# Values made token by token, and loaded through ScalarE's queue after the last weighted sums

## The reference, cut to what matters

```python
q = (xn @ wq + bq).reshape(b, n, H, HD).transpose(0, 2, 1, 3)    # H = HD = 16, k and v alike
fq, fk = jax.nn.elu(q) + 1.0, jax.nn.elu(k) + 1.0
kv = jnp.einsum('bhnd,bhne->bnde', fk, v)                         # per token n: 16 x 16
qkv = jnp.einsum('bhnd,bnde->bhne', fq, kv)
attn = qkv / (jnp.einsum('bhnd,bnd->bhn', fq, fk.sum(axis=1))[..., None] + 1e-06)
x = q_x + attn.reshape(b, n, c) @ wo + bo
return x + gelu(_ln(x) @ fc_w + fc_b) @ proj_w + proj_b
```

## Time and profile before

| | us |
|---|---|
| timed runs, median of 3 | 1108.08 |
| the profiled execution, its own time | 1103.53 |
| its span | 1101.4 |
| PE matmuls busy | 959.7 (87%) |
| DVE busy | 648.7 (59%) |
| ACT busy | 491.6 (45%) |
| GpSimd busy | 184.4 (17%) |
| DMA, mean over the 16 engines, queue of SP | 44.3% of the span, 353552 packets |
| DMA, queue of ACT | 2.9% of the span, 6656 packets |

### The profile page before, as it was taken

The page is one execution under the profiler, slowest core; times in us unless marked ns, Lnnn a source line. Parts: engine busy times, 40 slices in busy tenths (PEclk is TensorE's granted clock), DMA queues, the critical chain, the costliest instruction groups (busy, mean ns, idle before and its releaser), DMA issues.

```text
span 1101.4 us, 29193 instructions
## 1 busy us (share of the span) xinstructions
PE 959.7 (87%) x12208; PEld 716.9 (65%) x12208; DVE 648.7 (59%) x1557; ACT 491.6 (45%) x770; POOL 184.4 (17%) x113
## 2 busy tenths in 40 slices
PE   3755797989798989999999899999999899897966
PEld 1433685858595857777676758686776768685733
DVE  2433446565565666566667666766656765657433
ACT  1233354545354543646455444646464454342422
POOL 2020121121213121212121211211121210203000
PEclk9958699989898989999999999999999899898989
DMA  4556254545545453645555545637464535331023
GB/s 173 109 106 141 48 107 102 114 109 107 115 93 130 93 130 91 148 108 137 118 119 127 117 100 119 142 96 160 96 150 104 130 71 129 93 88 45 33 77 115
DMA packets 360343, 120.88 MB, mean 110 GB/s; under 512 B 325520, under 2 KB 342160, under 8 KB 359952
## 3 DMA queue, kind: packets, MB, share of 16 engines
q1 hardware_dynamic: 353552, 108.47, 44.3%
q10 hardware_dynamic: 6656, 10.50, 2.9%
HBM read 60.20 MB, written 58.72 MB: 108 GB/s over the span
## 4 chain that ended last, share of the span: by engine, by line
PE 64%; issue 10%; SPq 9%; DVE 8%; DMA 5%; ACT 2%; POOL 2%; ACTq 0%; DVEq 0%; POOLq 0%
PE pw L922 15%; PE pj L906 12%; PE ps L859 8%; PE ps L878 6%; SPq L338 6%; PE pw L832 5%; PE pj L832 4%; PE ps L891 4%; PE ps L970 3%; PE pw L859 3%; SPq L350 2%; PE pj L1014 2%; DMA scratch_nd<-ot 2%; DVE nd L679 1%; DVE am L650 1%
## 5 line engine op out<-in xcount | busy, mean ns | idle before, releaser
L922 PE MATMUL pw<-hT,w_fc 128*128 128x512 f32 x768 | 213.6, 419 | 11.1 <-DVE hT L670 11.1
L906 PE MATMUL pj<-w_pj,hidden 128*128 128x256 f32 x1536 | 208.4, 285 | 3.9 <-DVE hidden L663 3.9
L906 PEld LDWEIGHTS pj<-w_pj,hidden 128*128 128x128 f32 x1536 | 197.1, 189 | 15.3 <-DVE hidden L663 5.1
L505 ACT ACTIVATE xhT<-pw,col 128x512 f32<-128x512 f32 x128 | 88.0, 687 | 229.3 <-PE pw L922 227.9
L663 DVE TENSOR_TENSOR hidden<-xhT,hidden 128x512 fp32r<-128x512 f32 x128 | 88.5, 692 | 168.8 <-ACT hidden L506 168.8
L922 PEld LDWEIGHTS pw<-hT,w_fc 128*128 128x128 f32 x768 | 144.8, 200 | 44.0 <-DVE hT L670 12.8
L859 PE MATMUL ps<-xhT,w_qkv 128*128 128x512 f32 x256 | 126.1, 639 | 3.4 <-ACT xhT L459 3.2
L650 DVE TENSOR_TENSOR am<-ps,mask 128x512 f32<-128x512 f32 x128 | 79.4, 682 | 66.0 <-PE ps L878 66.0
L878 PE MATMUL ps<-kq 16*64 16x64 f32 x4096 | 89.2, 314 | 28.3 <-issue 15.2
L878 PEld LDWEIGHTS ps<-kq 16*64 16x64 f32 x4096 | 77.9, 209 | 50.9 <-issue 48.6
L859 PEld LDWEIGHTS ps<-xhT,w_qkv 128*128 128x128 f32 x256 | 51.4, 208 | 62.1 <-issue 60.4
(11 more groups left out here) (105 smaller groups left out, 1170.4 us busy)
## 6 DMA issues: line engine op xcount, KB each, us to landing
scratch_nd<-ot SPq DMA_DIRECT2D x32, 512.0 KB, 4.3
nd<-scratch_nd SPq DMA_DIRECT2D x96, 128.0 KB, 2.8
x_sb<-in_x SPq DMA_DIRECT2D x16, 512.0 KB, 5.8
scratch_v<-feat_v ACTq DMA_DIRECT2D x16, 512.0 KB, 3.8
scratch_q<-fqk SPq DMA_DIRECT2D x32, 256.0 KB, 3.6
scratch_k<-fqk SPq DMA_DIRECT2D x32, 256.0 KB, 4.7
kq<-scratch_q SPq DMA_DIRECT2D x128, 64.0 KB, 2.8
kq<-scratch_k SPq DMA_DIRECT2D x128, 64.0 KB, 2.8
```

The source lines that it names most:

```text
L505: nc.scalar.activation(gelub[:, u], pw[u], ACT.Gelu, bias=b_fc[:, m:m + 1])
L906: last = nc.tensor.matmul(pj[u][:, D * s:D * (s + 1)], hidden[:, m % SLOTS, a, lo:lo + P], w_pj[:, b, m], start=(m == 0 and n == 0 and s = ...
L922: last = nc.tensor.matmul(pw[bank], w_fc[:, b, c, P * m:P * (m + 1)], hT[:, a, c], start=(n == 0), stop=(n == len(order) - 1))
```

## The change

DV now puts 128 tokens on the partitions and 256 channels in the columns: 8 products of 256 columns in place of 4 of 512. DVE adds the bias as a row `bv`, made once by the new stage WV at the start, and ACT issues two stores. The row of a token in DRAM is chosen so that 8 DMAs of 1024 pieces of 64 bytes, issued by ACT, bring the values straight into `vb`. VL moves from SP's queue behind NS0 to ACT, between M3 (and NS1) and M4. VT, `vd` and their copies are gone. The DRAM buffer is doubled (`VRING`), and the weighted sums of round 1 wait for `v_in` on PE. In iteration 1, VL still stands ahead of DV; in iteration 2 it stands behind B3 and NS1.

```diff
-MERGED = ["L", "XS", "M1", "J2", "Y", "NS0", "VL", "M2", "NL0", "K0", "DS", "Z", "M3", "NS1", "D1", "M4", "NL1", "N0", "K1"]
+MERGED = ["L", "XS", "M1", "J2", "Y", "NS0", "M2", "NL0", "K0", "DS", "Z", "M3", "NS1", "VL", "D1", "M4", "NL1", "N0", "K1"]
-    yield 0, ["DS:0", "L:1", "D1", "X", "DV", ...
-    yield 1, ["X", "K0", "WS", "VL", "DV", "DQ", "DS:2", "DK", "D1:2", "B0", "B8", "VT", "K1"]
+    yield 0, ["WV", "DS:0", "L:1", "D1", "X", "DV", ...
+    yield 1, ["X", "K0", "WS", "VL", "DV", "DQ", "DS:2", "DK", "D1:2", "B0", "B8", "K1"]
...
 # SP
-                if p.stage == "VL":
-                    ...
-                    for j in range(NQ):
-                        for b in range(2):
-                            for v in range(2):
-                                sp.dma_start(vd[2 * j + b::2 * NQ]..., src[j, b, v]).then_inc(S["v_in"], 16)
 # ACT, stage DV
-                    for m in range(NC):
-                        wait(f"sa_full{m}", at(f"sa_full{m}", 1))
-                        nc.scalar.activation(feat_v[:, m], sa[m], ACT.Identity, bias=...).then_inc(S[f"sa_free{m}"], 1)
-                    act.dma_start(v_dram.rearrange("(c p) t -> p c t", p=P), feat_v[:, :, :]).then_inc(S["v_out"], 16)
+                    wait("v_in", at("v_in", -INC["v_in"]["VL"]))
+                    for u in range(2):
+                        wait(f"sa_free{u}", at(f"sa_free{u}", 1))
+                    dst = v_dram[p.t % VRING].rearrange("(g n b k) d -> b n g (k d)", g=2 * TA, n=2 * NQ, k=SUB)
+                    for b in range(2):
+                        act.dma_start(dst[b], feat_v[b::2].rearrange("p s d -> p (s d)")).then_inc(S["v_out"], 16)
+                if p.stage == "VL":
+                    wait("v_out", at("v_out"))
+                    for v in range(2):
+                        wait(f"sa_full{v}", at(f"sa_full{v}"))
+                    src = v_dram[p.t % VRING].rearrange("(g n) (h d) -> g h n d", g=2 * TA, d=HD)
+                    for v in range(2):
+                        for a in range(TA):
+                            act.dma_start(vb[BLOCK * v + a:BLOCK * (v + 1):TA, :, 0:HD], src[TA * v + a]).then_inc(S["v_in"], 16)
-                if p.stage == "VT":
-                    ...
 # DVE
+                if p.stage == "WV":
+                    dve.wait_ge(w_in[1], 16)
+                    for c in range(NC):
+                        last = nc.vector.tensor_copy(pb128[:, c], b_qkv[:, 2 * NC + c:2 * NC + c + 1].broadcast_to([P, P]))
+                    ...
+                    nc.vector.tensor_copy(bv[:, :], pw[0][:, 0:D]).then_inc(S["pw_free0"], 1)
+                if p.stage == "DV":
+                    ...
+                    for u in range(2):
+                        wait(f"sa_full{u}", at(f"sa_full{u}", 1))
+                        nc.vector.tensor_tensor(feat_v[:, 2 * u:2 * u + 2], sa[u].rearrange("p (s d) -> p s d", d=D),
+                                                bv[:, :].unsqueeze(1).broadcast_to([P, 2, D]),
+                                                ALU.add).then_inc(S[f"sa_free{u}"], 1)
 # PE
+                if p.stage == "DV":
+                    for u in range(2):
+                        wait(f"sa_free{u}", at(f"sa_free{u}"))
+                        for s in range(2):
+                            for c in range(NC):
+                                last = nc.tensor.matmul(sa[u][:, D * s:D * (s + 1)], xhT[:, c, 2 * u + s::SUB], w_qkv[:, 2, c],
+                                                        start=(c == 0), stop=(c == NC - 1))
+                        last.then_inc(S[f"sa_full{u}"], 1)
-                if p.stage == "VT":
-                    ...
-                            last = nc.tensor.transpose(pw[u][:, P * g:P * (g + 1)], vd[:, KG // 2 * u + g::KG], ident[:, :])
 # PE, round M1
-                        empty("pw")
+                        wait("v_in", at("v_in"))
                         weighted(0)
```

More of the change, by code:

```diff
@@ L22 @@
 X2RING = 1
+VRING = 2
 SLOTS = 4
@@ L58, in iterations @@
 def iterations():
[L60 to L62 removed]
+    yield 0, ["WV", "DS:0", "L:1", "D1", "X", "DV", "DS:1", "DQ", "L:2", "D1:1", "DK"]
+    yield 1, ["X", "K0", "WS", "VL", "DV", "DQ", "DS:2", "DK", "D1:2", "B0", "B8", "K1"]
+    yield 2, ["K0", "Y", "B1", "NS0", "X", "DV", "B2", "NL0", "DQ", "B3", "NS1", "VL", "NL1", "N0", "K1",
               "DK", "YB", "N", "A2", "R", "SA", "B0", "B8", "H"]
@@ L69, in iterations @@
         yield i, MERGED + (HEAD_TAIL if i % PER_BATCH == PER_BATCH - 1 else FULL_TAIL)
-    yield 16, ["XS", "M1", "J2", "Y", "NS0", "VL", "M2", "NL0", "K0", "Z", "M3", "NS1", "M4", "NL1", "N0", "K1", "XL",
-               "J7", "JA", "YB", "E", "VT", "N", "F1", "F3", "F4", "A2", "R", "SA", "B0", "B8", "H", "FX", "F2"]
+    yield 16, ["XS", "M1", "J2", "Y", "NS0", "M2", "NL0", "K0", "Z", "M3", "NS1", "VL", "M4", "NL1", "N0", "K1", "XL",
+               "J7", "JA", "YB", "E", "N", "F1", "F3", "F4", "A2", "R", "SA", "B0", "B8", "H", "FX", "F2"]
     yield 17, ["XS", "M1", "J2", "Y", "NS0", "M2", "NL0", "Z", "M3", "NS1", "M4", "NL1", "N0", "XL",
@@ L327, in run @@
                                          ).then_inc(S[f"{c}_out"], 16)
-                if p.stage == "VL":
[L329 to L334, removed]
-                    for j in range(NQ):
-                        for b in range(2):
-                            for v in range(2):
-                                sp.dma_start(vd[2 * j + b::2 * NQ].rearrange("p (v h t) -> p v h t", v=2, h=H)[:, v],
-                                             src[j, b, v]).then_inc(S["v_in"], 16)
                 if p.stage in ("K0", "K1"):
@@ L484, in run @@
                                              bias=b_qkv[:, j:j + 1]).then_inc(S[full.replace("full", "free")], 1)
-                if p.stage == "VT":
-                    for u in range(2):
-                        wait(f"pw_full{u}", at(f"pw_full{u}", 1))
-                        src = pw[u][:, :].rearrange("p (g d j) -> p j g d", d=HD, j=2 * NQ)
-                        dst = vb[:, :, :].rearrange("p (j g) e -> p j g e", j=2 * NQ)[:, :, KG // 2 * u:KG // 2 * (u + 1), 0:HD]
-                        nc.scalar.activation(dst, src, ACT.Identity).then_inc(S[f"pw_free{u}"], 1)
                 if p.stage == "H":
@@ L844, in run @@
                     last.then_inc(S["pw_full0"], 1)
+                if p.stage == "WV":
+                    wait("bv_ready", at("bv_ready", 1))
+                    for c in range(NC):
+                        last = nc.tensor.matmul(pw[0][:, P * c:P * (c + 1)], pb128[:, c], ident[:, :], start=True, stop=True)
+                    last.then_inc(S["pw_full0"], 1)
                 if p.stage == "X":
@@ L861, in run @@
                         last.then_inc(S[full], 1)
-                if p.stage == "VT":
-                    wait("v_in", at("v_in"))
-                    for u in range(2):
-                        wait(f"pw_free{u}", at(f"pw_free{u}"))
-                        for g in range(KG // 2):
-                            last = nc.tensor.transpose(pw[u][:, P * g:P * (g + 1)], vd[:, KG // 2 * u + g::KG], ident[:, :])
-                        last.then_inc(S[f"pw_full{u}"], 1)
                 def scores(b, part):
```

65 lines of the change are left out of this document (34 added, 31 removed).

## The result

The changed kernel takes 1187.14 us (median of 4 runs, 1181.42 to 1189.14) where the kernel before took 1108.16 beside it. The ratio is 1.0702, with a 95% interval from 1.0663 to 1.074. The forecast was 1117.5 with a range up to 1140, so the direction was right and the size far off. The span of the profiled execution grew from 1101.4 to 1184.3 us.

What follows compares the result with a forecast made beforehand. PE was taken to bound full iterations, with SP's value-load issues in the chain early on. The terms 28.0 - 7.9 - 2.0 - 5.0 - 3.7 gave +9.4 us, so 1117.5 us, range 1092 to 1140.

Steps and rivals of the forecast that it cites:

- V: Time of VL's 8 issues on ACT behind M3, taken as 5.4 us, with an upper end of about 7.3.
- s = V - 3.4: PE's stall in M4 from VL's issue time on ACT: 2.0 us in each of 14 rounds, +28.0 us.
- The rival of cheap issues: VL's 8 issues on ACT take 3.8 us, PE stalls 0.4 a round: -13 us, 1095; chance 0.33.
- The DMA-bound rival: DMA engines bound VL's issues: 7.3 us, PE stalls 3.9 a round, +36 us, 1144; chance 0.18.
- a few falls, 2 us each: Granted clock may fall after a short PE stall; a few falls, 2 us each, counted only in the DMA-bound rival.
- N takes 4.55 us as today: On DVE, N starts when JA ends, takes 4.55 us; first add ends 0.3 us ahead of DK's need; cost 0.
- The rival of a late division: VL's packets delay N's load, N starts 2 us late, DK waits for DVE's add: +4 us, 1112; chance 0.09.
- VT: Transposes taken off PE: 0.88 us in each of nine full iterations, -7.9 us.
- DV's weight loads: Twice as many on PE, each under a matmul of 256 columns: 0, at most +0.2 us a tile.
- Iterations 0 to 2: Mainly ACT's shorter wait before iteration 1's exponentials, 6.2 us: together -5 us, between -7 and -2.
- Iterations 3 to 6: DVE's 3.4 us wait for N's load goes, adds and stores take nearly all back: -0.5 each, -2 us.
- Iteration 16: N's wait of 3.98 us for its load goes, as the load comes earlier: -3.7 us.

Runs made afterwards that it cites:

- e2: Changed kernel with VL, still issued by ACT, moved from behind M3 to behind stage X; 1112.27 us, ratio 1.0112 to the kernel before.
- e3: Changed kernel with VL's 8 DMAs carrying 256 pieces each in place of 1024, three quarters of the values not loaded; 1144.75 us, ratio 1.0374.
- e10: Kernel before, plus 8 DMAs of 256 pieces of 64 bytes issued by ACT behind M3 into an unread tile; 1118.42 us, ratio 1.0136.
- e11: e2 with GpSimd's two additions of YB waiting until N is done; 1093.66 us, ratio 0.9925 to the kernel before.
- e9: e7 with DV's stationary operand read as 128 neighbouring tokens, not every fourth (result not computed correctly); 1085.62 us, ratio 0.9864.
- e7: Changed kernel with VL issued by ACT behind X and DV ahead of N on DVE; 1088.98 us, ratio 0.9873 to the kernel before.
- e12: e7 with VL in 2 DMAs and N kept ahead of DV in iterations 3 to 6; 1089.52 us, ratio 0.9875.
- e13: e7 with VL in 2 DMAs, DV ahead of N in iterations 3 to 6 too; 1082.97 us, ratio 0.9803.
- e8: Changed kernel with VL's 8192 pieces in 2 DMAs of 4096, same place and queue, each writing 64 neighbouring partitions; 1115.33 us, ratio 1.0092.
- e1: Changed kernel with VL's 8 DMAs issued by SP's queue at the same place of the list; 1119.19 us, ratio 1.0167.

## Why the prediction was wrong, step by step

**The step that failed is the size of V.** The formula s = V - 3.4 held over four kernels to 0.15 us (table above): the place, the run-ahead of ACT's sequencer, the 0.63 us of slack and PE's missing cover were all read rightly. V was taken as 5.4, between the old loads and the stores of queries and keys; it measured 8.0, above the upper end of 7.3. I had taken two prices as alternatives, one of issues (8 x 0.65) and one of packets (8192 at the engines' pace), and the larger as the bound. In the runs they come together: 6.2 us with a quarter of the pieces, 8.0 with all. The price of a packet itself was right: the 131072 packets of 64 bytes of the changed kernel have a median of 11 ns and a mean of 13.8 in the trace, and the 128-byte packets of the kernel before a mean of 13.3, so nothing doubled at 64 bytes. What failed was to let the larger of the two prices stand for both. The rival of cheap issues had V at 3.8 us, less than half of what it was. The DMA-bound rival had the right side and the wrong end, since a bound that assumes the queue takes up part of the work can't be the upper one. With 14 x 4.5 in place of 14 x 2.0 the sum would have been 35 us higher, 1152.5, which is half of the way to 1187.1. A slip stands beside it: with V = 5.2 and s = 1.8 the sum is 25.2 - 18.6 = +6.6 us, not +5.6. The 5.4 us of the same sentence take the price cited there as one per packet and engine, which the passage cited leaves open; the 11 ns measured here are per packet and engine.

**The clock was a term, not an accident.** I had priced "a few falls, 2 us each" in a rival alone, though the earlier trace rows showed that one follows PE's idle time. After against e2, which differ by the place of VL: the `down` products are busy 18.9 us longer (229.0 - 210.1), and the transposes (L823, three groups) 9.0 us longer. Over 14 rounds that is 2 us each, the very price I had, on every stall and not on a few. Shorter stalls at the same place were not always followed by the lower clock: those of 2.6 to 3.3 us in e3 were in 10 of 14 rounds, those of 0.4 to 2.0 us in e10 in 1 of 14. Idle time and clock together make 92 us; e2 waits and runs slowly elsewhere for 18 of them, and the spans differ by 74.6.

**DVE.** "N takes 4.55 us as today" was wrong: the work is the same, but its neighbour is not. From the earlier trace rows I read that N waited for a load; I did not look at what GpSimd did in that wait. N ended 2.85 us later than forecast, so the slack of 0.3 us became a wait at the DK products. It is 9.1 us in all, of which 1.6 fall in iteration 1; in six of the full iterations it is 1.1 us each, and in e2, without the stall, 1.9. The trace of the kernel before shows the collision too, in two of its 16 tiles, where N came beside the additions; that is why the mean of its group is 495 ns:

```profile
990.81 2.35 POOL L425 TENSOR_TENSOR x<-x,row 128x1024 f32<-128x1024 f32 x1 [23.80 <-DVE x_sb L715]
992.34 3.60 DVE L682 TENSOR_TENSOR nd<-nd 128x256 f32<-128x256 f32 x2
```

The rival of a late division named the right place, DK behind the addition, and the wrong cause: the load was early enough (N's wait for it is 1.5 us in the whole run). The Trainium skill ("SBUF — State Buffer", "Who interferes with whom") states that a DVE instruction with two inputs in SBUF contends with a GpSimd instruction that reads SBUF. The traces agree: 1.8 us a multiplication beside YB, 0.42 in e11 without it. The bias addition, which has one input in PSUM, took 0.68 both beside GpSimd (e11) and alone (here).

**VT** went as forecast: 0.9 us an iteration, and no L867 transposes. **DV's weight loads** were put at 0, at most 0.2 us a tile; they cost 0.38 where the clock is full (e9), about 4 us in ten tiles, because of a stride that the diff shows and the kernel before has nowhere on this operand.

**Iterations 0 to 2** gained more than the 5 us forecast. ACT starts the exponentials at 48.12, where 49.6 was worked out and 55.85 stood before. By JA of tile 0 the gain is 158.9 - 146.4 = 12.5 us in e2, and 6.1 in the changed kernel, which has one stall before that point. VL(0) itself takes 10.4 us of ACT's queue from 32.44, in time that ACT had. So 7.7 us are won at the exponentials, and 4.8 more arise in iterations 2 and 3, where the old VL no longer stands in SP's part of the chain. I had left these out; their place is read from the starts and was not tested by a run.

**Iterations 3 to 6** were to win 0.5 us each besides the stall; e2 has 175.8 where before had 170.6, a loss of 1.7 each. The collision takes 2.85 us of the 3.4 that the load gave back, and the stores and DQ's exponentials then follow the addition. With DV first (e7) the loss is gone, 170.6; e12 with N first has 175.7 there, e13 with DV first 172.7. **Iteration 16** was to win 3.7 us and the end wins 0.8: its multiplications take 3.60 us as well.

The parts sum up from tile to tile: -6.1 + 18.4 + 71.4 - 0.8 = +82.9 us, the whole difference of the spans. In the ten intervals of tiles 3 to 13 the stalls are 48.6 us, where the kernel before has 1.2, and the clock is some 20 (ten times 2). Less 9 for VT, plus 3 for DV and 7.5 for DK, that makes 69 of the 71.4.

## What to carry to other kernels

A DMA is issued by an instruction stream, and its issue time belongs to what that engine must do next. Put it where the engine has nothing in the bounding engine's loop for as long as the issues last: e2's issues take longer than the changed kernel's, and its span is 75 us shorter. Or make the issues short enough for the slack: e8, at the old place, gains as much. When a wait is removed, look at every engine that worked during it, since the work that now moves there has new neighbours. And when a stall of the bounding engine is priced, price the slower clock behind it with it.

## What the runs showed of the hardware that I had not expected

- The price of an issue depends on more than its pieces: 8 DMAs of 256 pieces of 64 bytes took 6.2 us (every fourth partition, e3) and 4.4 us (neighbouring partitions, another source, e10), and 2 of 4096 took 3.9. Eight of 1024 took 7.6 us on SP's queue (e1), 8.0 behind M3 and 9.3 behind X on ACT's. The Trainium skill ("DMA: Bandwidth & Descriptors", "Issuing engines are not separate DMA queues") calls this time "usually small relative to the DMA itself"; here a DMA's issue was 1.0 us and its landing 4.9, and the issues at their place were most of the loss.
- The lower clock is not bound to the start of the work behind a stall. In three of the 14 rounds it comes after PE has resumed (in iteration 10 PEclk is 1.00 from 608 to 612, while PE stands, and 0.68 and 0.50 behind). In the other eleven it comes while PE still stands, as here one iteration earlier, where PE resumes at 543.46:

```profile
541.00:543.00 2.00, 0.00 (x0) 0.00 (x0) 0.28 (x1) 1.58 (x3) 0.00 (x0) 0.51 1.60 138
```

- In a gate iteration G's two copies, too, take 2.50 us beside GpSimd's additions (e2) and 0.36 without them (e11): copies within SBUF on DVE are held up as the multiplications are.
